# Experts' second product with one 512-column matmul for two passes, the sum finished outside TensorE

## The chip, the cores and the metric

The kernel runs on one core of a Trainium2 chip. The metric is the device time of one execution in microseconds (us). Before the change it is 3690.21 us, the median of three runs (3688.73 to 3691.08). The change is judged by the same metric.

## What is computed

The input is 8 batches of 1024 rows of 256 numbers. Each row is normalised; an attention block gives `s`, a mixture of 8 experts (each row goes to its best two) gives `g`, and the output is `x + s * g`. This case touches the experts alone:

```
buf = zeros((E, capacity, H)).at[flat_e, slot].add(dispatched)
h = silu(einsum('ech,ehf->ecf', buf, w1))
out_buf = einsum('ecf,efh->ech', h, w2)
pair_out = out_buf[flat_e, slot] * keep
```

with E = 8 experts, H = 256 and F = 1024.

## The kernel before

**Two parts for each number.** Products are made in a fast 32-bit format (fp32r) that keeps fewer bits. So each operand is split into a high part (the rounded value) and a low part (the rest), and each product is three matmuls: high by high, high by low, low by high. `PASSES` lists the three.

**Groups.** The rows of all experts are cut into 71 groups of 256 rows (`GROUPS`, `GP`), each of one expert. Groups are numbered from 0; "a" below is the group whose first product runs. Every engine has its own program, and they meet through semaphores.

- TensorE (`tensor`, `body`, lines 1834 to 1893): for group a the first product `hidden(a)` (48 matmuls of 256 columns into four banks `phid`), then `turn(a+1)` (four transposes of the next group's rows), then the second product of the group before, `down(a-1)`, again 48 matmuls of 256 columns: two row tiles c, eight pieces f of the inner dimension, three passes. They sum up in the first 256 columns of the two banks `po`. `down` first waits (line 1853) until the sums of the group before have been taken out of `po` (`s_oe`).
- ScalarE, ACT (`scalar`, `body`, line 1803): `high1(a+1,0)` makes the high part of half of the next w1, four times `silu(a,j)` (two instructions each), `high1(a+1,1)`, and `high2(a+1,0)`, `high2(a+1,1)` for w2. `high1` waits for the load of w1 (`s_w1`), `high2` for `down(a-1)`.
- VectorE, DVE (`vector`, `body`, line 1728): `low1(a+1,0)`, four times `hidden(a,j)` (the low part of the silu's result), `turned(a+1)` (two instructions on the transposes), `low1(a+1,1)`, `outputs(a-1)` (line 1723: copies `po` to `out`, raises `s_oe`), `low2(a+1,0)`, `low2(a+1,1)`.
- GpSimd, POOL (`gpsimd`, line 1641) issues all DMAs of this stage, in a fixed order: for group g two scatters of the results of group g-4 to DRAM (`scatter(g - LAG)`, LAG = 4, which waits for `s_oe`), the load of w1 of g (1 MB), two gathers of the rows of g, the load of w2 of g (1 MB). An indirect DMA costs POOL itself about a microsecond, in which it makes the DMA's descriptors.

**The order of POOL's steps for one group:**

```
for g in range(GROUPS):
    if g >= LAG:
        scatter(g - LAG)             # waits for s_oe >= g - LAG + 1
    if g >= 2:
        e.wait_ge(s_w1l, 2 * (g - 1))
    weights(g, io["w1"], raw1[q], s_w1[q])
```

**The end.** After the loops, ACT and DVE already make the parts of the attention's first output pieces (`first_piece`, lines 1752 to 1766 and 1819 to 1824), as their loads land; TensorE runs `hidden(70)`, `down(69)`, `down(70)` and the first products of the next phase.

Of the kernel before, what the change touches and what calls it, by code (L numbers as in the profile page):

```python
# [24 lines left out]
P = 128  # L25
NBATCH, S, D = 8, 1024, 256
# [56 lines left out]
class Phase:  # L83
# [5 lines left out]
    def sb(self, name, shape, dt=F32):  # L89
        return self.ctx.enter_context(self.nc.sbuf_tensor(f"{self.tag}_{name}", shape, dt))  # L90
# [1462 lines left out]
def expert_parts(nc, ctx, bridge, io, scr, keep, seam):  # L1553


    with ExitStack() as tiles:
# [18 lines left out]
        w1[1] = sb("w11", [P, HL, NF, KD, P], F32R)  # L1575
        w2[1] = sb("w21", [P, HL, NF, D], F32R)
        hT[1] = sb("hT1", [P, HL, NF, GP], F32R)
        phid = ps("h", [P, NQ, HALF])
        ptr = ps("tr", [P, KD, HALF])
        po = ps("o", [P, GT, HALF])  # L1580
# [1 line left out]
        s_rows = sem("rows")  # L1582
        s_slots, s_tr, s_xh, s_xT, s_h, s_silu, s_hT, s_o, s_oe = (sem(n) for n in ("slots", "tr", "xh", "xT", "h", "act", "hT", "o", "oe"))
        s_w1h, s_w1l, s_w2h, s_w2l = (sem(n) for n in ("w1h", "w1l", "w2h", "w2l"))
        s_wo, s_wh, s_wl = (sem(n) for n in ("wo", "wh", "wl"))

        def half1(tile, k):
            return tile[:, k * (W // 2):(k + 1) * (W // 2)]
# [10 lines left out]
        def groups(e, body, after=None):  # L1599

            for g in range(3):
                body(At(0, g))
                if after:
                    after(g)
            with e.Fori(1, (GROUPS - 1) // 2 - 1) as it:
                for off in (1, 2):
                    body(At(it, off))

        def first_piece(q):

# [104 lines left out]
        def vector(e, after):  # L1715
            low1, low2, turned = vector_steps(e)

            def hidden(a, j):
                fs = slice(2 * j, 2 * j + 2)
                e.wait_ge(s_silu, a.n(2 * NQ, 2 * j + 2))  # L1720
                e.tensor_tensor(out=hT[a.u][:, 1, fs, :], in0=hs[:, fs, :], in1=hT[a.u][:, 0, fs, :].bitcast(F32), op=ALU.subtract).then_inc(s_hT, 1)

            def outputs(a):
                wait(e, s_os[a.u], a.same(16 * GT))
                e.wait_ge(s_o, a.n(1, 1))
                e.tensor_copy(out[a.u][:, :, :], po[:, :, 0:D]).then_inc(s_oe, 1)  # L1726

            def body(a, first=False):
                one = a.next(1)
                if first:  # L1730
                    turned(one)
                low1(one, 0)
                for j in range(NQ):
                    hidden(a, j)
                if not first:
                    turned(one)
                low1(one, 1)
                if not first:
                    outputs(a.next(-1))
                low2(one, 0)  # L1740
                low2(one, 1)

            groups(e, lambda a: body(a, isinstance(a.base, int) and a.off == 0), after)
            body(At(0, GROUPS - 2))
            last = At(0, GROUPS - 1)
            e.wait_ge(s_wh, 1)
            e.tensor_tensor(out=wo[1][:, :, :], in0=wraw, in1=wo[0][:, :, :].bitcast(F32), op=ALU.subtract).then_inc(s_wl, 1)
            for j in range(NQ):
                hidden(last, j)
            outputs(last.next(-1))  # L1750

            def low(q):
                src, hi, lo = first_piece(q)
                e.wait_ge(seam["oh"], q + 1)
                e.tensor_tensor(out=lo, in0=src, in1=hi.bitcast(F32), op=ALU.subtract).then_inc(seam["ol"], 1)

            for q in range(TB // 2):
                low(q)
                if q == 2:
                    e.wait_ge(s_o, GROUPS)  # L1760
                    wait(e, s_os[last.u], last.same(16 * GT))
                    e.tensor_copy(out[last.u][:, 0, :], po[:, 0, 0:D]).then_inc(s_oe, 1)
            e.wait_ge(s_o, GROUPS + 1)
            e.tensor_copy(out[last.u][:, 1, :], po[:, 1, 0:D]).then_inc(s_oe, 1)
            for q in range(TB // 2, TB):
                low(q)

# [23 lines left out]
        def scalar(e):  # L1791
            high1, high2 = scalar_steps(e)

            def silu(a, j):
                fs = slice(2 * j, 2 * j + 2)
                e.wait_ge(s_h, a.n(NQ, j + 1))
                wait(e, s_hT, a.n(NQ, j + 1 - NQ))
                if j == 0:
                    wait(e, s_o, a.n(1, -1))
                e.activation(hT[a.u][:, 0, fs, :].rearrange("p f s -> p (f s)"), phid[:, j, :], ACT.Silu).then_inc(s_silu, 1)  # L1800
                e.activation(hs[:, fs, :].rearrange("p f s -> p (f s)"), phid[:, j, :], ACT.Silu).then_inc(s_silu, 1)  # L1801

            def body(a):
                one = a.next(1)
                high1(one, 0)
                for j in range(NQ):
                    silu(a, j)
                high1(one, 1)
                high2(one, 0)
                high2(one, 1)  # L1810

            groups(e, body)
            body(At(0, GROUPS - 2))
            e.wait_ge(s_wo, 16)
            e.activation(wo[0][:, :, :], wraw, ACT.Copy).then_inc(s_wh, 1)
            for j in range(NQ):
                silu(At(0, GROUPS - 1), j)
            e.wait_ge(s_h, NQ * (GROUPS - 1))
            for q in range(TB):
                if q == TB // 2:  # L1820
                    e.wait_ge(s_o, GROUPS - 1)
                e.wait_ge(seam["o"][q // 2], 16)
                src, hi, lo = first_piece(q)
                e.activation(hi, src, ACT.Copy).then_inc(seam["oh"], 1)
# [9 lines left out]
        def tensor(e, after, emptied):  # L1834
            def hidden(a, after=None):
                q = a.u
                e.wait_ge(s_xT, a.n(1, 1))
                for j in range(NQ):
                    if j % 2 == 0:
                        e.wait_ge(s_w1l, a.n(2, j // 2 + 1))  # L1840
                    wait(e, s_silu, a.n(2 * NQ, 2 * j + 2 - 2 * NQ))
                    for f in (2 * j, 2 * j + 1):
                        for ws, xs in PASSES:
                            for k in range(KD):
                                mm = e.matmul(phid[:, j, f % 2 * GP:(f % 2 + 1) * GP], w1[q][:, ws, f, k, :], xT[q][:, xs, k, :],  # L1845
                                              start=(ws + xs + k == 0), stop=(ws == 1 and k == KD - 1))
                    mm.then_inc(s_h, 1)
                    if j == 0 and after:
                        after()

            def down(a, halves=False):
                q = a.u
                wait(e, s_oe, a.n())
                for c in range(GT):
                    for f in range(NF):
                        if c == 0 and f % 2 == 0:
                            e.wait_ge(s_hT, a.n(NQ, f // 2 + 1))
                        if c == 0 and f % (NF // 2) == 0:
                            e.wait_ge(s_w2l, a.n(2, f // (NF // 2) + 1))
                        for hh, ws in PASSES:  # L1860
                            mm = e.matmul(po[:, c, 0:D], hT[q][:, hh, f, c * P:(c + 1) * P], w2[q][:, ws, f, :],  # L1861
                                          start=(hh + ws + f == 0), stop=(hh == 1 and f == NF - 1))
                    if halves and c == 0:
                        mm.then_inc(s_o, 1)
                mm.then_inc(s_o, 1)

            def body(a):
                first = isinstance(a.base, int) and a.off == 0
                if first:
                    turn(e, a.next(1))  # L1870
                hidden(a, after if first else None)
                if not first:
                    turn(e, a.next(1))
                if first:
                    emptied()
                else:
                    down(a.next(-1))

            groups(e, body)
            body(At(0, GROUPS - 2))  # L1880
            last = At(0, GROUPS - 1)
            hidden(last)
            down(last.next(-1))
            down(last, True)
            e.wait_ge(s_silu, 2 * NQ * GROUPS)
            e.wait_ge(s_wl, 1)
            for t in range(READY):
                if t % 2 == 0:
                    e.wait_ge(seam["ol"], t + 2)
                for r in range(HP):  # L1890
                    for os, ws in PASSES:
                        e.matmul(seam["pj"][t][:, 0:D], seam["oT"][0][os][:, r, t * P:(t + 1) * P], wo[ws][:, r, :],
                                 start=(os + ws + r == 0), stop=(os == 1 and r == HP - 1))
# [421 lines left out]
```

## Time and profile before

| | us |
|---|---|
| median of three runs | 3690.21 |
| the profiled execution's own time | 3694.65 |
| its span (first to last instruction) | 3693.1 |
| PE busy | 3626.7 (98%) |
| DVE busy | 3198.4 (87%) |
| ACT busy | 2773.1 (75%) |
| POOL busy | 1198.0 (32%) |
| mean granted clock of TensorE | 0.997 of full speed |

The experts' stage lies between about 2650 and 3500 us from the span's start. In a row of the timeline the columns are the start, the duration, the engine, the line, the operation, what is written and read, the shape, and how many instructions were merged; behind them, in brackets, how long the engine was idle before and what ended that. PE stands for matmuls, PEld for TensorE's weight loads.

### The profile page before, as it was taken

To read this page: it belongs to the slowest core of one execution; us is meant where nothing else is said; L and a number is where in the kernel's file an instruction comes from. 1 tells how busy PE (TensorE), PEld (TensorE's weight loads), DVE (VectorE), ACT (ScalarE), POOL (GpSimd) and SP (SyncE) were. 2 spreads that over 40 slices of the span, in tenths; PEclk is the share of its full clock that TensorE was granted. 3 is DMA by queue.
4 is the path that set the end of the run, shared out by engine and by line. 5 is a ranking of instruction groups with operands and counts; after the bars stand their busy time and mean duration, and the time that the engine had idled before them with its cause. 6 is when DMAs were issued, how large, how long until landed. Compare 5 with 4: busy or idle time off the path is not lost. (4 is left out here: it accounts for less than half of the span.)

```text
span 3693.1 us, 76388 instructions
## 1 busy us (share of the span) xinstructions
PE 3626.7 (98%) x23848; PEld 2352.4 (64%) x23848; DVE 3198.4 (87%) x4340; ACT 2773.1 (75%) x4016; POOL 1198.0 (32%) x1178
## 2 busy tenths in 40 slices
PE   6989999999999999999999999999999999999999
PEld 5754444444444444444444444444699999999998
DVE  8868999999999999999999989999777777777799
ACT  5767888888888888887888888888766666666665
POOL 2202222222222222222222222223366666666400
PEclk9999999999999999999999999999999999999999
DMA  7975666666666666666666666665566666666798
GB/s 261 358 262 136 175 167 173 170 168 171 163 174 160 181 160 181 155 183 157 180 160 174 166 173 170 166 170 147 169 218 224 219 214 216 224 214 216 234 370 274
DMA packets 378435, 724.72 MB, mean 196 GB/s; under 512 B 105277, under 2 KB 253886, under 8 KB 342272
## 3 DMA queue, kind: packets, MB, share of 16 engines
q0 software_dynamic: 83504, 340.66, 35.8%
q1 hardware_dynamic: 292816, 382.71, 31.3%
q10 hardware_dynamic: 2048, 0.53, 0.1%
q8 instruction: 34, 0.56, 0.1%
q14 instruction: 33, 0.27, 0.0%
HBM read 453.60 MB, written 138.81 MB: 160 GB/s over the span
## 5 line engine op out<-in xcount | busy, mean ns | idle before, releaser
L1161 ACT ACTIVATE at_ex<-at_st 128x1024 f32<-128x1024 f32 x1024 | 1049.7, 1026 | 114.6 <-PE at_st L1326 101.3
L1339 PE MATMUL at_pv<-at_ex,at_v 128*64 128x512 f32 x4096 | 991.6, 605 | 0.0
L1019 DVE TENSOR_REDUCE at_mx<-at_fr 128x1 f32<-128x512 f32 x1024 | 705.4, 689 | 238.1 <-PE at_fr L1349 195.6
L1185 ACT ACTIVATE at_fr<-at_fr 128x512 f32<-128x512 f32 x1024 | 602.7, 589 | 290.2 <-PE at_fr L1349 244.9
L1339 PEld LDWEIGHTS at_pv<-at_ex,at_v 128*64 128x64 f32 x4096 | 248.4, 136 | 478.4 <-issue 463.0
L1032 DVE TENSOR_TENSOR at_sum<-at_sum,at_ex 128x1024 f32<-128x1024 f32 x448 | 544.9, 1216 | 3.7 <-ACT at_ex L1161 2.4
L1349 PE MATMUL at_fr<-at_kfar,at_qh 64*128 64x512 f32 x1024 | 460.0, 449 | 5.5 <-DVE at_mx L1019 5.0
L1346 PE MATMUL at_fr<-at_kdif,at_qh 64*128 64x512 f32 x1024 | 460.3, 449 | 3.5 <-DVEq L674 2.5
L1346 PEld LDWEIGHTS at_fr<-at_kdif,at_qh 64*128 64x128 f32 x1024 | 188.1, 184 | 416.4 <-issue 362.7
L1861 PE MATMUL ex_o<-ex_w,ex_hT 128*128 128x256 f32 x3408 | 426.0, 285 | 0.9 <-DVE ex_out L1726 0.9
L1845 PE MATMUL ex_h<-ex_xT,ex_w 128*128 128x256 f32 x3408 | 421.1, 283 | 1.8 <-ACT ex_hs L1801 1.5
L1845 PEld LDWEIGHTS ex_h<-ex_xT,ex_w 128*128 128x128 f32 x3408 | 414.1, 192 | 3.0 <-issue 2.6
L1861 PEld LDWEIGHTS ex_o<-ex_w,ex_hT 128*128 128x128 f32 x3408 | 413.2, 192 | 1.1 <-DVE ex_out L1726 1.1
L1326 PE MATMUL at_st<-at_qh,at_kh 64*128 64x512 f32 x2048 | 407.4, 394 | 5.4 <-DMA at_top<-at_mneg 5.1
L1326 PE MATMUL at_st<-at_ql,at_kh 64*128 64x512 f32 x2048 | 402.7, 389 | 0.0
L1326 PE MATMUL at_st<-at_qh,at_kl 64*128 64x512 f32 x2048 | 402.6, 389 | 0.0
L920 POOL DMA_DIRECT2D at_rotq<-at_swpq x126 | 111.4, 1031 | 842.2 <-DVE at_swpq L987 841.5
L1779 ACT ACTIVATE ex_w<-seam_stage 128x1024 fp32r<-128x1024 f32 x142 | 142.6, 1051 | 286.1 <-PE ex_o L1861 286.1
L1651 POOL DMA_INDIRECT scr_eo<-ex_out,mid_slots x142 | 253.2, 1783 | 215.6 <-DVE ex_out L1726 179.6
L1032 DVE TENSOR_TENSOR at_sum<-at_ex 128x1024 f32<-128x1024 f32 x224 | 272.4, 1216 | 1.7 <-ACT at_ex L1161 1.7
L914 POOL DMA_DIRECT2D at_sum<-at_sum x95 | 88.5, 931 | 519.2 <-DVE at_sum L1032 495.1
L1326 PEld LDWEIGHTS at_st<-at_qh,at_kl 64*128 64x128 f32 x2048 | 193.1, 185 | 45.6
(208 smaller groups left out, 6119.7 us busy)
## 6 DMA issues: line engine op xcount, KB each, us to landing
at_cq<-scr_c SPq DMA_DIRECT2D x62, 1024.0 KB, 6.3
at_ck<-scr_c SPq DMA_DIRECT2D x62, 1024.0 KB, 5.1
at_sum<-at_sum POOLq DMA_DIRECT2D x95, 512.0 KB, 6.1
scr_v<-pj_v SPq DMA_DIRECT2D x64, 512.0 KB, 6.9
at_v<-scr_v SPq DMA_DIRECT2D x64, 512.0 KB, 6.6
mid_rec<-scr_rec SPq DMA_DIRECT2D x256, 128.0 KB, 3.0
scr_o<-mid_oT SPq DMA_DIRECT2D x64, 512.0 KB, 3.1
at_rotq<-at_swpq POOLq DMA_DIRECT2D x126, 256.0 KB, 4.8
```

The costliest lines, as they stand in the source:

```text
L1019: e.reduce_max(mx[k // QB][:, h * QB + k % QB:h * QB + k % QB + 1], fr[h][:, :], AX.X).then_inc(s_tr[h], 1)
L1032: e.tensor_tensor(out=acc, in0=ex[k - 1][:, :, :] if first else acc, in1=ex[k][:, :, :], op=ALU.add).then_inc(s_sum, 1)
L1161: e.activation(ex[k][:, :, :], st[u % 2][:, :, :], ACT.Exp, scale=SCALE).then_inc(s_exp, 1)
L1185: e.activation(fr[h][:, :], fr[h][:, :], ACT.Relu).then_inc(s_pos[h], 1)
L1326: mm = e.matmul(st[u % 2][:, h, :], kk[rows[h], :] if t == 3 else kk[rows[h], keys], qq[rows[h], bank[n]], start=(t == 0 and kt < 2), stop ...
L1339: mm = e.matmul(pv[n][rows[h], :], v[i.u][:, kt, rows[h]], ex[kt][:, h, :], start=(kt == 0), stop=(kt == KT - 1))
L1346: return e.matmul(fr[h][:, :], query_tile(j, k, h), kdif[j.u][rows[h], :], start=True, stop=True)
L1349: return e.matmul(fr[h][:, :], query_tile(j, k, h), kfar[j.u][rows[h], :], start=False, stop=True, skip_group_check=True)
L1651: e.indirect_dma_start(out=scr["eo"], out_offset=bass.IndirectOffsetOnAxis(ap=slots[:, g * GT + c:g * GT + c + 1], axis=0), in_=out[g % 2] ...
L1779: e.activation(w2_half(a.u, 0, k), half2(raw2[a.u], k), ACT.Copy).then_inc(s_w2h, 1)
L1845: mm = e.matmul(phid[:, j, f % 2 * GP:(f % 2 + 1) * GP], w1[q][:, ws, f, k, :], xT[q][:, xs, k, :], start=(ws + xs + k == 0), stop=(ws == ...
L1861: mm = e.matmul(po[:, c, 0:D], hT[q][:, hh, f, c * P:(c + 1) * P], w2[q][:, ws, f, :], start=(hh + ws + f == 0), stop=(hh == 1 and f == NF ...
```

## The change

The operands of two passes, high by high and high by low, share the stationary side (the silu's high part). They become one matmul of 512 columns: the two parts of w2 side by side as the moving operand, into all 512 columns of a `po` bank. The third pass goes on adding to the first 256 columns. The 256 columns of high by low now have to be added afterwards: ACT copies them to a new tile `rest` (`rests`), and DVE's copy to `out` becomes an addition of `po`'s first half and `rest`. `outputs` waits for a new semaphore `s_rest` instead of `s_o`, and both steps have another place: `rests(a-2)` runs on ACT in the body of a, between `silu(a,0)` and `silu(a,1)`, and `outputs(a-2)` on DVE just after `hidden(a,0)`. Before, `outputs(a-1)` stood at the end of the body of a, ahead of `low2(a+1,0)`. POOL's program is not touched.

```
+        def older(a):
+            return not isinstance(a.base, int) or a.n() >= 2
             def outputs(a):
                 wait(e, s_os[a.u], a.same(16 * GT))
-                e.wait_ge(s_o, a.n(1, 1))
-                e.tensor_copy(out[a.u][:, :, :], po[:, :, 0:D]).then_inc(s_oe, 1)
+                e.wait_ge(s_rest, a.n(1, 1))
+                e.tensor_tensor(out=out[a.u][:, :, :], in0=po[:, :, 0:D], in1=rest[:, :, :], op=ALU.add).then_inc(s_oe, 1)
...
                 for j in range(NQ):
                     hidden(a, j)
+                    if j == 0 and older(a):
+                        outputs(a.next(-2))
                 if not first:
                     turned(one)
                 low1(one, 1)
-                if not first:
-                    outputs(a.next(-1))
                 low2(one, 0)
...
             for j in range(NQ):
                 hidden(last, j)
+                if j == 0:
+                    outputs(last.next(-2))
             outputs(last.next(-1))
...
+            def rests(a, c=slice(0, GT), done=1):
+                wait(e, s_oe, a.n(1, done - 1))
+                e.wait_ge(s_o, a.n(1, done))
+                e.activation(rest[:, c, :], po[:, c, D:], ACT.Copy).then_inc(s_rest, 1)
...
                 for j in range(NQ):
+                    if j == 1 and older(a):
+                        rests(a.next(-2))
                     silu(a, j)
...
             for q in range(TB):
                 if q == TB // 2:
-                    e.wait_ge(s_o, GROUPS - 1)
+                    rests(last.next(-1))
+                if q == TB // 2 + 2:
+                    rests(last, slice(0, 1))
+                if q == TB // 2 + 3:
+                    rests(last, slice(1, 2), 2)
...
-                        for hh, ws in PASSES:
-                            mm = e.matmul(po[:, c, 0:D], hT[q][:, hh, f, c * P:(c + 1) * P], w2[q][:, ws, f, :],
-                                          start=(hh + ws + f == 0), stop=(hh == 1 and f == NF - 1))
+                        cols = slice(c * P, (c + 1) * P)
+                        e.matmul(po[:, c, :], hT[q][:, 0, f, cols], w2[q][:, :, f, :], start=(f == 0), stop=(f == NF - 1))
+                        mm = e.matmul(po[:, c, 0:D], hT[q][:, 1, f, cols], w2[q][:, 0, f, :], start=False, stop=(f == NF - 1), skip_group_check=True)
```

The last group's two row tiles are likewise copied and added one by one, and an unused tile of 928 numbers a partition is put ahead of `rest`.

## Rows read from the trace of the kernel before

**Rows 1.** The page, costliest groups: instructions, busy us, mean ns, idle before.

```profile
L1861 PEld LDWEIGHTS ex_o<-ex_w,ex_hT 128*128 128x128 f32 x3408 | 413.2, 192 | 1.1 <-DVE ex_out L1726 1.1
```

**Rows 2.** Sums of one stretch: length, each engine's busy time (instructions), clock, DMA.

```profile
2700.00:3460.00 760.00, 760.00 (x6360) 760.00 (x6359) 584.25 (x698) 496.06 (x764) 499.41 (x381) 1.00 0.63 218
```

**Rows 3.** Waits, 2690 to 3470 us: who for whom, total us, times, longest.

```profile
POOL scr_eo L1651 <- DVE ex_out L1726: 168.2, 66, 2.7
```

**Rows 4.** Timeline of all engines, one group's round, group 30.

```profile
3000.53 5.92 PE L1845 MATMUL ex_h<-ex_xT,ex_w 128*128 128x256 f32 x48
3000.73 2.01 ACT L1779 ACTIVATE ex_w<-seam_stage 128x1024 fp32r<-128x1024 f32 x2 [4.16 <-PE ex_o L1861]
3000.73 0.69 DVE L1726 COPY ex_out<-ex_o 128x512 f32<-128x512 f32 x1 [1.92 <-PE ex_o L1861]
3001.82 2.36 DVE L1683 TENSOR_TENSOR ex_w<-seam_stage,ex_w 128x1024 fp32r<-128x1024 f32 x2 [0.40 <-ACT ex_w L1779]
3002.26 1.67 POOL L1651 DMA_INDIRECT scr_eo<-ex_out,mid_slots  x1 [2.57 <-DVE ex_out L1726]
3002.64 1.04 ACT L1773 ACTIVATE ex_w<-seam_stage 128x1024 fp32r<-128x1024 f32 x1
3003.59 0.57 ACT L1800 ACTIVATE ex_hT<-ex_h 128x512 fp32r<-128x512 f32 x1
...
3004.10 1.22 DVE L1679 TENSOR_TENSOR ex_w<-seam_stage,ex_w 128x1024 fp32r<-128x1024 f32 x1
3004.23 1.95 POOL L1651 DMA_INDIRECT scr_eo<-ex_out,mid_slots  x1 [0.30 <-issue]
3004.55 0.59 ACT L1800 ACTIVATE ex_hT<-ex_h 128x512 fp32r<-128x512 f32 x1
3005.02 0.61 ACT L1801 ACTIVATE ex_hs<-ex_h 128x512 f32<-128x512 f32 x1
3005.23 2.09 DVE L1721 TENSOR_TENSOR ex_hT<-ex_hs,ex_hT 128x512 fp32r<-128x512 f32 x3
...
3006.49 0.98 POOL L1643 DMA_INDIRECT seam_stage<-in_w,keep_widx  x1 [0.30 <-issue]
3006.62 5.82 PEld L1861 LDWEIGHTS ex_o<-ex_w,ex_hT 128*128 128x128 f32 x48
...
3007.61 0.69 DVE L1721 TENSOR_TENSOR ex_hT<-ex_hs,ex_hT 128x512 fp32r<-128x512 f32 x1 [0.28 <-ACT ex_hs L1801]
3007.77 1.37 POOL L1666 DMA_INDIRECT mid_xg<-scr_xn,mid_rows  x1 [0.30 <-issue]
...
3009.55 1.21 DVE L1679 TENSOR_TENSOR ex_w<-seam_stage,ex_w 128x1024 fp32r<-128x1024 f32 x1
3010.70 0.95 POOL L1643 DMA_INDIRECT seam_stage<-in_w,keep_widx  x1 [0.30 <-issue]
...
3014.59 1.05 ACT L1773 ACTIVATE ex_w<-seam_stage 128x1024 fp32r<-128x1024 f32 x1
```

**Rows 5.** Timeline of PE alone: matmuls of 512 columns, back to back.

```profile
207.32 1.52 PE L1423 MATMUL at_fr<-at_cq,at_kdif 128*128 128x512 f32 x6
208.68 1.52 PE L1385 MATMUL at_pv<-at_ck,at_wk 128*128 128x512 f32 x6
```

**Rows 6.** Line 1643, issue to landing: all 2700 to 3470, then w1's of Rows 4.

```profile
DMA to landing us min/median/max: 5.3/5.5/7.9
DMA to landing us min/median/max: 5.5/5.5/5.5
```

**Rows 7.** Timeline of DVE, the low parts of group 2.

```profile
2673.49 2.53 DVE L1721 TENSOR_TENSOR ex_hT<-ex_hs,ex_hT 128x512 fp32r<-128x512 f32 x4
```

**Rows 8.** Timeline of the stage's end: outputs(69), down(70), ACT's third and fourth piece.

```profile
3490.45 0.69 DVE L1726 COPY ex_out<-ex_o 128x512 f32<-128x512 f32 x1 [2.98 <-PE ex_o L1861]
...
3491.19 5.81 PEld L1861 LDWEIGHTS ex_o<-ex_w,ex_hT 128*128 128x128 f32 x48 [1.06 <-DVE ex_out L1726]
...
3492.60 2.01 ACT L1824 ACTIVATE seam_oT<-seam_stage 128x1024 fp32r<-128x1024 f32 x2 [1.11 <-DMA seam_stage<-scr_o]
```

More of the change, by code:

```diff
@@ L1577, in expert_parts @@
         hT[1] = sb("hT1", [P, HL, NF, GP], F32R)
+        sb("past_sums", [P, 928])
+        rest = sb("rest", [P, GT, D])
         phid = ps("h", [P, NQ, HALF])
@@ L1584, in expert_parts @@
         s_w1h, s_w1l, s_w2h, s_w2l = (sem(n) for n in ("w1h", "w1l", "w2h", "w2l"))
-        s_wo, s_wh, s_wl = (sem(n) for n in ("wo", "wh", "wl"))
+        s_wo, s_wh, s_wl, s_rest = (sem(n) for n in ("wo", "wh", "wl", "rest"))
         def half1(tile, k):
@@ L1759, in vector @@
                 if q == 2:
-                    e.wait_ge(s_o, GROUPS)
                     wait(e, s_os[last.u], last.same(16 * GT))
-                    e.tensor_copy(out[last.u][:, 0, :], po[:, 0, 0:D]).then_inc(s_oe, 1)
-            e.wait_ge(s_o, GROUPS + 1)
-            e.tensor_copy(out[last.u][:, 1, :], po[:, 1, 0:D]).then_inc(s_oe, 1)
+                    e.wait_ge(s_rest, GROUPS)
+                    e.tensor_tensor(out=out[last.u][:, 0, :], in0=po[:, 0, 0:D], in1=rest[:, 0, :], op=ALU.add).then_inc(s_oe, 1)
+            e.wait_ge(s_rest, GROUPS + 1)
+            e.tensor_tensor(out=out[last.u][:, 1, :], in0=po[:, 1, 0:D], in1=rest[:, 1, :], op=ALU.add).then_inc(s_oe, 1)
             for q in range(TB // 2, TB):
@@ L1815, in scalar @@
             e.activation(wo[0][:, :, :], wraw, ACT.Copy).then_inc(s_wh, 1)
+            last = At(0, GROUPS - 1)
             for j in range(NQ):
-                silu(At(0, GROUPS - 1), j)
+                if j == 1:
+                    rests(last.next(-2))
+                silu(last, j)
             e.wait_ge(s_h, NQ * (GROUPS - 1))
```

## Prediction

> **What bounds the kernel now.** I read four views. The page's costliest groups show the second product's weight loads, 192 ns each, with 1.1 us of idle time before them in the whole run [rows 1]. The sums over 2700 to 3460 us show PE busy for all 760 us at full clock, while DVE is busy for 584, ACT for 496 and POOL for 499 [rows 2]. So in the experts' stage PE alone sets the pace; its count of instructions and their spacing are the time. The waits show who has room: POOL waits 66 times, 2.5 us each, for the copy on line 1726 [rows 3]. The timeline of one round shows the rest [rows 4]: ACT's `high1(a+1,0)` starts at 3002.64 and that of the next group at 3014.59, so a round is 11.95 us. Two chains cross a round with little room. First, `outputs` to scatter to w1's load to `high1`: w1 of group a+2 is issued at 3006.49, lands 5.5 us later [rows 6] at 11.96, and is wanted at 14.59; room 2.6 us. Second, `outputs` to `down`.
>
> **What the change takes from PE.** 48 loads of `down` last 5.82 us; less the last one's own 0.19, over 47 steps, that is 0.120 us a matmul of 256 columns [rows 1, 4]. Matmuls of 512 columns on full 128x128 weights start every (208.68 - 207.32)/6 = 0.227 us [rows 5]. Three matmuls of 0.120 become 0.227 + 0.120: 0.347 in place of 0.360 us, 0.013 less, as one change of weights goes and the columns stay 768. There are 16 such triples a group and 71 groups: 0.21 us a round, 15.1 us in all. That the moving operand now comes in two runs of 256 is not in any row; bounds are no gain at all (two steps of 0.120, near which it would only come if the split cost 13 ns) and the 0.227. I take the 0.227, the same shape. If PE stayed the bound, a round would be 11.74 us.
>
> By the Trainium skill, "TensorE: Matmul & The Clock Gate", section "Back-to-back issue gap", a warm matmul takes N/2.4 + 2.5 ns, so 109 and 216 ns. The rows have 120 and 227, about 11 ns more each. By the page the merger would save 2.5 ns a triple, 2.8 us in all.
>
> **What it adds.** ACT: one copy of 128x512 a round. Its neighbours of that size start 0.48 apart (3004.55, 3005.02) [rows 4]. It runs beside PE, and ACT idles 4.16 us a round [rows 4]: nothing by itself. DVE: the addition reads `po` and `rest`; the copy took 0.69 us, and like-sized additions last 0.69 too (3007.61) [rows 4]; nothing. `rests` waits for `s_o` of a `down` that ended before `high2`, so it never blocks ACT. It starts 0.95 us after `silu(a,0)` does and is done before DVE comes to the addition (below).
>
> **What it moves, and who is queued behind.** `outputs(a-2)` ran at 3000.73, right after `down(a-2)`. It now runs behind `low2`, `low1(a+1,0)` and `hidden(a,0)`. `hidden(a,0)` starts at 3005.23, and steps of DVE of this size follow one another after 0.60 us ((2.53 - 0.69)/3 with a first wait left out, [rows 7]). So the addition starts at 3005.83, 5.1 us later than the copy. Call this moment O.
> - PE's `down(a-1)` waits for its end, O + 0.69 + 0.05 = 3006.57 (0.05: end of the copy 3491.14 to PEld 3491.19 [rows 8]), plus the sequencer's steps behind the wait. PE gets there at 3006.62: a delay of 0 to 0.2 us a round, at most 14 us.
> - POOL's scatter waits for it too, and in POOL's program w1's load of group a+2 stands behind the two scatters. Here the 5.1 us meet a room of 2.6. This is where the time goes.
>
> **The new loop.** `outputs(n)` releases `scatter(n)`, behind it w1 of n+4 is loaded, `high1(n+4,0)` waits for it on ACT, `silu(n+3,0)` is queued behind `high1`, `hidden(n+3,0)` on DVE waits for both, and the next thing on DVE is `outputs(n+1)`. Once around per group, independent of PE. From O:
> - the addition, 0.69; to POOL's scatter 3002.26 - 3001.42 = 0.84 [rows 4]: O + 1.53.
> - POOL's own time. An indirect DMA takes 0.95 us when DVE is idle (3010.70). The scatters took 1.67 and 1.95 and the gather 1.37 [rows 4]. The excess of each is just the time until DVE's running operation on two SBUF tiles is over: 3002.26 to the second `low2` at about 2.96 is 0.70; 4.23 to 5.23 is 1.00; 7.77 to 8.21 is 0.44. So I lay POOL against DVE's new order. ACT's `high1` starts at O - 2.83 (below); silu pairs follow 0.95 after it and 0.95 apart, with 0.48 for `rests` after the first pair, and the second pair's result is there 1.1 us after its start: O + 0.66. So `hidden(a,1)` starts near O + 0.69, (2) near 1.67, (3) near 2.64 (the same steps on), each for 0.60. The first scatter (O + 1.53) meets none: 0.97. The next starts 0.30 after, O + 2.80, and waits for `hidden(a,3)` until 3.24: ends 4.19. w1's load starts at O + 4.50. `low1(a+1,1)`, which would hold it for 1.14 us, follows `hidden(a,3)` by 9.55 - 7.61 = 1.94 [rows 4], at O + 4.58: 0.08 us too late to catch it.
> - landing 5.5 [rows 6]: O + 10.00. To ACT's start 0.1: bounded by 0.03 (ACT to DVE) and 0.84 (DVE to POOL), near the first, as a compute engine waits.
> - `high1` to `low1` on DVE 1.09 (3000.73 to 3001.82), `low1` to `hidden(.,0)` 1.13, to the addition 0.60 [rows 4]: 2.83.
>
> Sum: 4.50 + 5.5 + 0.1 + 2.83 = 12.93 us, more than 11.74. The loop is the bound, and PE's gain and the added work vanish in its room.
>
> **The sum.** `outputs(0)` comes with group 2, at 2673.49 + 0.60 = 2674.09 [rows 7]. 67 loops lead to `outputs(67)`: 2674.09 + 67 x 12.93 = 3540.4. `down(68)` follows after 0.69 + 0.15 at 3541.2; before, it started 39 rounds after `down(29)`, the one in rows 4 (3006.62 + 39 x 11.95 = 3472.8). Later by 68.4. Behind it `down(68)` is 0.2 shorter. At the end `rests(69)` stands behind ACT's fourth piece, while the copy of 69 did not: the pieces start at 3492.60, wait for a load and take 1.9; `rests(69)` 3494.5 to 3495.1, addition to 3495.85, `down(70)` at 3495.9 in place of 3491.19 [rows 8]: 4.7 later (`down(69)` waits too, for `outputs(68)`, but less than this covers). Together 72.9: 3694.65 + 72.9 = 3767.6 for an execution like the profiled one, which is 4.4 above the median of the runs. So 3763 us.
>
> **The rivals.**
> 1. *A longer loop.* POOL is caught once more, by `low1(a+1,1)` (margin 0.08 us) or by `hidden(a,2)`: 1.1 us more, 14.0 a round, 67 x 1.07 = 72 more: 3835. For it: the margins are thin; some loads took up to 7.9 to land [rows 6].
> 2. *A shorter loop.* The second scatter isn't caught (margin 0.16 us): 12.4 to 12.5, 3690.2 + 36 + 4.5 = 3731.
> 3. *Faster: w1's load still lands in time.* One mechanism: the loop stays below 11.74, PE remains the bound. Then 15.1 less, the end's 4.7 more, some 2 for `down` behind `outputs`: 3682. It decides at 1.2 us less than my sum. Against it: with POOL never caught (3.5 to 4.0 up to w1) and the shortest landing of 5.3 the loop is still 12.2.
> 4. *No change: a quick landing.* If w1 landed 1.1 us sooner, in 4.4, the loop would be 11.83 and the time 3690. No load of line 1643 took under 5.3 [rows 6]. The 4.4 us is what the Trainium skill gives for 1 MB, "DMA: Bandwidth & Descriptors", section "Anatomy of one DMA — SWDGE (gpsimd) path" (2.0 us and the bytes at 436 GB/s); by that rule the change would cost nothing; the trace disagrees by 1.1 us.
> 5. *PE's clock falls* in the 1.2 us it now idles a round. At the lower of its two levels for a third of its work PE would need 3.9 us more, and could become the bound at 15.7 a round: 67 x 2.7 = 181 more, 3944. Clock is 1.00 in the stretch [rows 2]; nothing there speaks for it.
>
> **How the numbers follow.** Forecast 0.45, longer loop 0.25, shorter 0.18, faster 0.05, no change 0.03, clock 0.04. The range takes in the first three: 3724 to 3842. A measurement of this kernel can tell about 0.2% from no change: faster 0.05, same 0.03, slower 0.92.
>
> **What would show it.** After the change ACT should wait at line 1773 for w1's load, 1.2 us or more in each round; PE should idle as much a round, ahead of `down`, released by line 1726's successor on DVE; POOL's wait for DVE should be there still, and the rounds in the timeline be 12.9 apart. 512-column matmuls should start 0.227 apart. The chain is wrong if w1 lands before ACT wants it; only the sizes are if ACT waits but the round isn't 12.9.

## The result, and the profile after

The changed kernel takes 3772.9 us (median of 4 runs, 3772.2 to 3775.7) where the kernel before takes 3690.6 on the same chip: 1.0221 times as long, with a 95% interval of 1.0209 to 1.0233. It is 82 us slower, though TensorE has less to do. The profiled execution took 3772.2 us with a span of 3770.6; that of before 3694.65 and 3693.1. The difference of the two spans, 77.5 us, is what the traces can account for.

In the changed kernel the lines have moved: `outputs` is L1731, the hidden layer's low parts L1726, `low1` L1684, `low2` L1688, `high1` L1780, `high2` L1786, `rests` L1813, the scatters L1656, the loads of w1 and w2 L1648, the second product L1882 (512 columns) and L1883 (256).

The sums over the stretch of [rows 2], 2700 to 3460 us (length; busy time of PE, PEld, DVE, ACT, POOL with instructions; clock; share and GB/s of the DMA engines):

```profile
2700.00:3460.00 760.00, 702.78 (x4881) 647.73 (x4880) 539.32 (x640) 487.03 (x755) 403.97 (x349) 1.00 0.56 199
```

PE was busy for all 760 us before and is now idle for 57 of them. Every engine does less in the same time: DVE 539 instead of 584, POOL 404 instead of 499. No engine has become the bound; they all wait for one another. The waits of 2690 to 3540 us (who for whom: us in all, times, longest), which answer to [rows 3]:

```profile
POOL scr_eo L1656 <- DVE ex_out L1731: 297.2, 65, 5.7
...
ACT ex_w L1780 <- DMA seam_stage<-in_w,keep_widx: 81.2, 60, 2.5
DVE ex_w L1684 <- ACT ex_w L1780: 65.3, 62, 3.4
PE ex_o L1882 <- DVE ex_out L1731: 61.7, 62, 2.5
```

The last three are new (among the eight longest waits of before, over 2690 to 3470 us, there is none of ACT for w1's load, none of DVE for `high1` and none of PE for `outputs`), and they are one chain: ACT waits for w1's load, DVE for ACT, PE for DVE. POOL in turn waits for DVE, and issues w1's load behind that; so the chain bites its own tail. One turn of it in the timeline, DVE, POOL, ACT and PE put together as in [rows 4] (start, duration, engine, line, in brackets the idle time before and what ended it). `outputs` runs at 3000.46 and again at 3013.28:

```profile
3000.46 0.68 DVE L1731 TENSOR_TENSOR ex_out<-ex_o,ex_rest 128x512 f32<-128x512 f32 x1
...
3001.98 1.01 POOL L1656 DMA_INDIRECT scr_eo<-ex_out,mid_slots  x1 [4.37 <-DVE ex_out L1731]
3003.29 1.38 POOL L1656 DMA_INDIRECT scr_eo<-ex_out,mid_slots  x1 [0.30 <-issue]
3004.97 0.98 POOL L1648 DMA_INDIRECT seam_stage<-in_w,keep_widx  x1 [0.30 <-issue]
...
3005.05 1.21 DVE L1684 TENSOR_TENSOR ex_w<-seam_stage,ex_w 128x1024 fp32r<-128x1024 f32 x1
...
3010.45 1.06 ACT L1780 ACTIVATE ex_w<-seam_stage 128x1024 fp32r<-128x1024 f32 x1 [1.12 <-DMA seam_stage<-in_w,keep_widx]
...
3013.28 0.68 DVE L1731 TENSOR_TENSOR ex_out<-ex_o,ex_rest 128x512 f32<-128x512 f32 x1
...
3014.21 0.47 PE L1882 MATMUL ex_o<-ex_w,ex_hT 128*128 128x512 f32 x1 [0.73 <-DVE ex_out L1731]
```

From `outputs` to w1's load 4.51 us, to ACT's `high1` 5.48, to `outputs` again 2.83: 12.82. The room of 2.6 us between w1's landing and ACT's need of it, read from [rows 4, 6], is gone, and ACT has 1.12 us of idle time in its place. Over the 67 turns of the stage the four legs have these medians and means: `outputs` to the start of w1's load 4.51 and 4.57 us, landing 5.52 and 5.60, landing to `high1` 0.10 and 0.07, `high1` to `outputs` 2.84 and 2.85. The means sum to 13.09, which is (3546.03 - 2669.15)/67.

### The profile page after: what moved, and what is told of

Same layout as the page of the kernel before. It is cut to its first block and busy times, and to the rows that moved or that the text cites. A ratio compares the mean times of both kernels' runs of the same rounds, so it can differ in the third digit from the quotient of the medians.

```text
span 3770.6 us, 74292 instructions
## 1 busy us (share of the span) xinstructions
PE 3638.8 (97%) x22712; PEld 2297.1 (61%) x22712; DVE 3203.0 (85%) x4340; ACT 2815.2 (75%) x4088; POOL 1134.1 (30%) x1178
## 5 line engine op out<-in xcount | busy, mean ns | idle before, releaser
L1882 PE MATMUL ex_o<-ex_w,ex_hT 128*128 128x512 f32 x1136 | 413.1, 406 | 69.2 <-DVE ex_out L1731 69.2
L1883 PE MATMUL ex_o<-ex_w,ex_hT 128*128 128x256 f32 x1136 | 320.3, 282 | 0.0
L1786 ACT ACTIVATE ex_w<-seam_stage 128x1024 fp32r<-128x1024 f32 x142 | 142.7, 1052 | 231.0 <-PE ex_o L1883 231.0
L1882 PEld LDWEIGHTS ex_o<-ex_w,ex_hT 128*128 128x128 f32 x1136 | 215.9, 190 | 133.2 <-issue 45.3
L1688 DVE TENSOR_TENSOR ex_w<-seam_stage,ex_w 128x1024 fp32r<-128x1024 f32 x142 | 167.8, 1222 | 150.2 <-ACT ex_w L1786 150.2
L1656 POOL DMA_INDIRECT scr_eo<-ex_out,mid_slots x142 | 169.9, 1197 | 361.6 <-DVE ex_out L1731 323.0
```

Source lines behind the costliest of these rows:

```text
L1656: e.indirect_dma_start(out=scr["eo"], out_offset=bass.IndirectOffsetOnAxis(ap=slots[:, g * GT + c:g * GT + c + 1], axis=0), in_=out[g % 2] ...
L1882: e.matmul(po[:, c, :], hT[q][:, 0, f, cols], w2[q][:, :, f, :], start=(f == 0), stop=(f == NF - 1))
L1883: mm = e.matmul(po[:, c, 0:D], hT[q][:, 1, f, cols], w2[q][:, 0, f, :], start=False, stop=(f == NF - 1), skip_group_check=True)
```

## The experiments

Two theories stood against each other. *The loop*: the later `outputs` closes a loop over POOL's fixed order, w1's load and DVE, which no engine's work sets; the merged product is harmless. *The work*: the rounds are longer because ACT's copy, the addition and the wider matmul cost more than they save. Each kernel's time is a median beside the kernel before on its own chip, which was at 3690.1 (for the first four of the table), 3689.8 (the next four) and 3692.8 (the last two); so compare the ratios across chips, not the times. "Round" is the median from one hidden layer's first matmul to the next; that of before is 11.953 us.

| kernel | us | ratio, 95% interval | round, us |
|---|---|---|---|
| moved, not merged | 3806.4 | 1.0315 [1.0298, 1.0333] | 13.593 |
| merged, not moved | 3686.8 | 0.9992 [0.9982, 1.0001] | 11.847 |
| changed, w1's load halved | 3707.3 | 1.0045 [1.0028, 1.0061] | 12.013 |
| changed, scatters a group later | 3693.5 | 1.0007 [0.9997, 1.0017] | 11.954 |
| changed, a fill on POOL | 3836.5 | 1.0397 [1.0378, 1.0416] | 14.076 |
| before, the same fill | 3689.5 | 0.9998 [0.9988, 1.0008] | 11.953 |
| merged, not moved, w2 side by side | 3686.1 | 0.9992 [0.9983, 1.0001] | 11.847 |
| merged, not moved, earlier last copy | 3683.0 | 0.9980 [0.9971, 0.9989] | 11.847 |
| changed, w1's load ahead of the scatters | 3699.6 | 1.0015 [1.0005, 1.0025] | 11.921 |
| as the row "earlier last copy", matmuls grouped | 3683.2 | 0.9970 [0.9960, 0.9981] | 11.787 |

**Only the move.** The kernel before, with nothing changed but the place of `outputs`:

```
                 for j in range(NQ):
                     hidden(a, j)
+                    if j == 0 and (not isinstance(a.base, int) or a.n() >= 2):
+                        outputs(a.next(-2))
...
                 low1(one, 1)
-                if not first:
-                    outputs(a.next(-1))
```

> The kernel before with nothing but the place of the copy changed: outputs(a-2) right after hidden(a,0) on DVE; no 512-column matmul, no rest. Loop theory (the copy's late place delays scatter and with it the load of w1): slow, without any of the new arithmetic. Laid out as in the prediction, without ACT's extra copy hidden(a,1) to (3) come 0.1 to 0.5 us earlier against O, the first scatter is caught by hidden(a,2) until O+1.8, w1's load starts at O+4.36 and is caught by low1(a+1,1) until O+5.17: loop 13.6 to 13.7 us, time 3805 to 3815, slower than the changed kernel itself. If DVE's running operation doesn't hold POOL (rival on the size): loop 12.9 to 13.1, 3765 to 3773. Rival (the cost is the new work: 512 columns out of two runs, the extra ACT copy, two inputs for DVE): 3690 to 3700.

Measured 3806.4: the move alone costs 116 us, more than the whole change. So the merged product, ACT's copy and the addition don't lengthen the rounds; in the new place they even shorten them by 0.66 us (13.593 to 12.935). POOL's and DVE's timeline of this kernel shows why (`outputs` is L1726 here and had started 4.37 us before the load, `low1` is L1679):

```profile
3001.80 1.22 DVE L1679 TENSOR_TENSOR ex_w<-seam_stage,ex_w 128x1024 fp32r<-128x1024 f32 x1
...
3002.07 1.79 POOL L1643 DMA_INDIRECT seam_stage<-in_w,keep_widx  x1 [0.30 <-issue]
```

Here `low1` starts 0.27 us ahead of w1's load, and the load takes POOL 1.79 us in place of 0.98, until `low1` is over. The landing, counted from the load's start, has a median of 6.31 us in place of 5.52: 0.79 more. In the changed kernel ACT's copy after the first silu pair holds up the pairs behind it by 0.48 us, and with them `hidden(a,1)` to `hidden(a,3)` and `low1` on DVE, which then comes 0.08 us after the load. By these rows an added operation on ACT made the round shorter; no run adds the copy alone.

**Only the merge.** The changed kernel with `rests` behind `high1(a+1,1)` and `outputs` where it was before:

```
                 for j in range(NQ):
-                    if j == 1 and older(a):
-                        rests(a.next(-2))
                     silu(a, j)
                 high1(one, 1)
+                if older(a.next(1)):
+                    rests(a.next(-1))
```

> The changed kernel with the merged matmul, the copy to rest and the addition, but the latter two in the old place (outputs(a-1) ahead of low2(a+1,0), rests(a-1) just ahead of high2(a+1,0)). Loop theory: PE is the bound again, 11.74 us a round: 15 us less than before, plus some 4 at the end (rests(69) behind ACT's fourth piece): 3680, ratio 0.997. If the merged matmul saves nothing: 3695. Rival (the new work costs the time): 3770 as after the change.

The loop is open: every round takes 11.847 us, PE is busy for 760 of 760 us. But the gain per round is 0.106 us and not 0.21, and the end loses 6.0 us: from the last hidden layer to the first matmul of the next product it is 24.4 us, 18.4 before. Both were followed up below. What is left of the time, 3.3 us less than before, can't be told from nothing: the interval takes in 1.

**A microsecond on POOL inside the loop.** A fill of a spare tile, from group 8 on, in both kernels:

```
                     scatter(g - LAG)
+                if g > 8:
+                    e.wait_ge(s_slots, 16 + g - 8)
+                if g >= 8:
+                    e.memset(spare[:, :], 0.0).then_inc(s_slots, 1)
                 if g >= 2:
```

> The changed kernel with one POOL fill of a spare tile of 928 columns (about 1.2 us with its gap, an estimate) between the two scatters and the load of w1, from group 8 on; the output is unchanged. Theory 'loop outputs, scatters, w1 load, landing, high1, low1, hidden, outputs': every microsecond on POOL between the scatters and the load is on the loop: a round of 13.09 + about 1.2 = 14.3, 62 rounds, 3772.9 + 75 = 3848 (3825 to 3870, since the size of the fill is an estimate). Rival 'the rounds are longer because DVE, ACT or the DMA queues carry more': POOL has 13.09 - 4.9 us free in a round, the fill is hidden, 3773.

> The kernel before with the same fill at the same place, which separates its price as work from its price on the loop. Theory: the loop isn't closed there (the w1 load is early by more than a microsecond against its reader), 3690 and a round of 11.95. Rival: it lengthens the rounds here too, by up to 1.2 us each, 3765; then the change didn't put the load on the path, it was there before.

The fill takes 0.89 us. Rows of the changed kernel, POOL's and DVE's, and POOL's of the kernel before:

```profile
3009.56 0.89 POOL L1666 MEMSET ex_past_sums<- 128x928 f32 x1
...
3009.93 1.21 DVE L1688 TENSOR_TENSOR ex_w<-seam_stage,ex_w 128x1024 fp32r<-128x1024 f32 x1
...
3010.61 1.39 POOL L1648 DMA_INDIRECT seam_stage<-in_w,keep_widx  x1 [0.16 <-issue]
```

```profile
3004.64 0.89 POOL L1662 MEMSET ex_spare<- 128x928 f32 x1
3005.69 0.99 POOL L1644 DMA_INDIRECT seam_stage<-in_w,keep_widx  x1 [0.16 <-issue]
```

The fill follows the second scatter at once, and 0.16 us lie behind it where 0.30 lay between scatter and load. So it puts the load off by 0.89 + 0.16 - 0.30 = 0.75 us in both kernels (median from `outputs` to the load 5.26 in place of 4.51, and 6.51 in place of 5.76). In the changed kernel the later load also meets `low1`, and takes POOL 1.39 us in place of 0.98. The two together are 1.16, and the median round grew by 1.14. In the kernel before the same 0.75 us are free: 3689.5, round 11.953 to the nanosecond. So the stretch of POOL's program between `outputs` and w1's load is on the path after the change, and was not before.

The time grew by 63.6 us (3836.5 - 3772.9), near what 62 fills of 1.05 us would give, but that isn't how it came about: 63 turns have a fill, 47 us of fills in all, and the load caught by `low1` in 61 of them adds 25 more. Against that the profiled execution of this kernel lacks most of the late turns of the changed kernel, described further below. The forecast's 3848 had 1.2 us for the fill and left the catch out.

**Half the load.** The changed kernel, w1's load cut to half its bytes from group 4 on (its first half then holds other rows' numbers and the rest is stale, so the output is wrong; order and waits stay):

```
-                weights(g, io["w1"], raw1[q], s_w1[q])
+                if g < 4:
+                    weights(g, io["w1"], raw1[q], s_w1[q])
+                else:
+                    weights(g, io["w1"].rearrange("r (h c) -> (r h) c", h=2), raw1[q][:, 0:W // 2], s_w1[q])
```

> The changed kernel with w1's load halved from group 4 on (the first half of the tile alone is loaded, with wrong rows, and the rest keeps an older group's numbers); order and waits stay. Loop theory: landing falls from 5.5 to about 3.6 us, the loop to about 11.0, under PE's 11.74: 3680 to 3692. Rival (the landing is not in the loop; PE, ACT or DVE themselves are slower): 3770.

It lands 1.5 us sooner (median of the 24 loads whose landing is recorded and that `low1` didn't hold: 3.98), and 65 of the 82 us come back, so the landing is a leg of the loop. But 3707 was not in the forecast of 3680 to 3692. The turns alternate between 11.86 to 11.97 and 12.1 to 12.3. POOL's and DVE's rows of a long one:

```profile
3011.54 1.22 DVE L1687 TENSOR_TENSOR ex_w<-seam_stage,ex_w 128x1024 fp32r<-128x1024 f32 x1
...
3011.81 1.80 POOL L1648 DMA_INDIRECT seam_stage<-in_w,keep_widx  x1 [0.30 <-issue]
```

With the loop shorter, `low1` again starts ahead of the load and lengthens it by 0.8 us, in every second round. A halved load also lands in 3.98 and not in 3.6.

**The loop opened by a later scatter.** The changed kernel with the scatters one group later (`LAG` 5 in place of 4), which frees w1's load from the group's `outputs`:

```
-        HL, LAG = 2, 4
+        HL, LAG = 2, 5
```

> The changed kernel with LAG = 5: POOL scatters the group before the one it scatters now, so that it never waits for the moved addition; all arithmetic and the late place stay. Loop theory: the loop is cut, PE is the bound at 11.74 plus 0 to 0.2 for down behind outputs: 3676 + 0 to 14 + 4 at the end, 3680 to 3692, centre 3685. Rival (PE waits for the late addition, or the new work costs): 3770.

All but 3.4 us of the 82 come back, PE is busy for 760 of 760 us again. The round's mean is 11.925, 0.08 above that of "only the merge": between a hidden layer's last matmul and the second product's first there are 590 ns in place of 475, the wait behind the late `outputs`. The rest is one long round at the start (16.1 us) and 4.3 us at the end, so it came out a little above the forecast.

**The loop opened by POOL's order.** The changed kernel, each load of w1 ahead of the scatters:

```
             for g in range(GROUPS):
                 q = g % 2
-                if g >= LAG:
-                    scatter(g - LAG)
                 if g >= 2:
                     e.wait_ge(s_w1l, 2 * (g - 1))
                 weights(g, io["w1"], raw1[q], s_w1[q])
+                if g >= LAG:
+                    scatter(g - LAG)
```

> The changed kernel, where POOL issues each load of w1 ahead of the two scatters instead of behind them; copy and addition stay where the change put them. Theory 'the loop runs through POOL's order': the load of w1 no longer waits for outputs of the group, so it starts 4 to 5 us earlier against its reader, the loop is open by far more than the 1.1 us it was too long, and the rounds go back to TensorE's work, 11.85, with at most 0.1 us for the late outputs; with the end's +4, 3685 to 3697, centre 3692. Rival 'outputs is late because of what stands ahead of it on VectorE, whatever POOL does': the round stays at 13 and the time at 3773.

```profile
3005.22 0.94 POOL L1648 DMA_INDIRECT seam_stage<-in_w,keep_widx  x1 [0.30 <-issue]
```

The load starts 2.9 us ahead of `outputs` (3008.14) instead of 4.5 behind it; `high1` no longer waits for it, and the round is 11.92. So DVE's order by itself, which is that of the changed kernel, costs 0.07 us a round, not 1.1. The kernel is still 0.15% slower than before: the late `outputs` (613 ns in place of 475 ahead of each second product), a first long round (2.9 us more) and the end (3.9 us more) outweigh the 0.106 us a round that the merge saves. The forecast's 3697 at most was for a chip on which before takes 3690; by the ratio this is 3695.7.

**Why 0.106 us and not 0.21.** In "only the merge" the 512-column matmul takes 236 ns from start to start (median of 1136; most are 232 to 241) and the 256-column one 117, together 353 (in the changed kernel, where the loop is the bound, the median is 233), where [rows 5] had given 227 + 120. Two causes were tried. First, w2's parts side by side, so that the 512 columns are one run (`w2` as `[P, NF, HL, D]` in place of `[P, HL, NF, D]`):

```
-        w2[0] = sb("w20", [P, HL, NF, D], F32R)
+        w2[0] = sb("w20", [P, NF, HL, D], F32R)
...
-            return half2(w2[q][:, s, :, :].rearrange("p f d -> p (f d)"), k)
+            return w2[q][:, k * (NF // 2):(k + 1) * (NF // 2), s, :]
...
-                        e.matmul(po[:, c, :], hT[q][:, 0, f, cols], w2[q][:, :, f, :], start=(f == 0), stop=(f == NF - 1))
+                        e.matmul(po[:, c, :], hT[q][:, 0, f, cols], w2[q][:, f, :, :], start=(f == 0), stop=(f == NF - 1))
```

> The kernel with the merged product and everything else in its old place (3686.8 us, round 11.847 us), with w2's two parts of one block of rows laid side by side on chip, so that the 512 columns that a matmul streams are one contiguous run instead of two runs of 256. In that kernel and in the changed one the 512-column matmul takes 234 to 241 ns from start to start, where the stage before it had 227. Theory 'the split operand costs it': 227 ns again, a round of 11.74, some 70 rounds x 0.11 = 7.5 us less, 3679. Rival 'it is the neighbour' (a 256-column matmul in between, a new weight load for each): 236 ns and 3687 as before. What would speak for a third case: ScalarE's and VectorE's operations on w2 longer than 0.96 and 1.14 us per half because their output is now in pieces.

Nothing changed: 236 and 117 ns, a round of 11.847. The split of the operand is free. Second, the order of the matmuls, tried together with the earlier last copy of the next experiment:

```
                         e.matmul(po[:, c, :], hT[q][:, 0, f, cols], w2[q][:, :, f, :], start=(f == 0), stop=(f == NF - 1))
+                    for f in range(NF):
                         mm = e.matmul(po[:, c, 0:D], hT[q][:, 1, f, cols], w2[q][:, 0, f, :], start=False, stop=(f == NF - 1), skip_group_check=True)
```

> The kernel with the merged product in the old place and the earlier last copy (3683.0, round 11.847), where in each column of tiles the eight 512-column matmuls go first and the eight 256-column ones behind them, instead of in turn. It tells what makes the 512-column matmul take 236 ns from start to start instead of the 227 ns of the stage before. Theory 'changing between the two widths costs it': 227 and 120 ns, 0.347 per triple, round 11.74, 70 x 0.107 = 7.5 us less, 3675.5. Rival 'a 512-column matmul that writes two runs of the accumulator with a new weight load costs 236 ns anyway, and the 256 one behind it gets 3 ns back': 0.356 per triple, a round of 11.9, 3686.

It fell between the two: 231 ns (median, 226 to 236) among 512-column ones, 120 for the others, a round of 11.787. So the alternation costs about 4 ns of the 6 or 7 missing per triple (0.060 us by 16 triples); what the other 3 are for stays open. The time is 3683.2 against 3692.8, the best ratio of the study (0.9970); against the 0.9980 of the earlier last copy alone the intervals overlap.

**The end.** In "only the merge" the copy of the second half of `outputs(69)` stands on ScalarE behind four pieces of the next product, and runs at 3485.55:

```profile
3483.64 2.00 ACT L1841 ACTIVATE seam_oT<-seam_stage 128x1024 fp32r<-128x1024 f32 x2 [1.02 <-DMA seam_stage<-scr_o]
...
3486.23 0.69 DVE L1731 TENSOR_TENSOR ex_out<-ex_o,ex_rest 128x512 f32<-128x512 f32 x1 [6.19 <-ACT ex_rest L1811]
```

Moved ahead of the third piece:

```
             for q in range(TB):
-                if q == TB // 2:
+                if q == 2:
                     rests(last.next(-1))
```

> The kernel with everything in its old place (3686.8), where the 6.0 us that it loses after the last hidden layer come from the copy of the second half of outputs(69), which stands on ScalarE behind four pieces that wait for transfers (copy at 3485.55, addition at 3486.23 after 6.19 us idle, down(70) behind it). Here that copy stands ahead of the third piece: down(69) ends at 3482.2, copy 3482.4 (or at 3482.6, behind the second piece), addition 3483.1 to 3483.3, down(70) from 3483.9 instead of 3487.0. Theory: 3.1 us come back, 3683.7. Rival: the first product's pieces end last anyway, nothing comes back, 3687; if all 6.0 were that one copy, 3681.

3683.0. On the same chip "w2 side by side", which has the rounds of "only the merge", took 3686.1, 3.1 us more; the two intervals just overlap. `outputs(69)` now comes 12.4 us after the last hidden layer's start in place of 15.5, the 3.1 us foreseen, and the next product's first matmul 18.8 in place of 24.4. Why 5.6 us there are worth only some 3 in the time stays open. This version is faster than the kernel before by 0.2% (interval 0.1 to 0.3%).

## Why the prediction was right, point by point

**The verdict and its mechanism.** 3763 us was forecast, 3724 to 3842, slower with 0.92; 3772.9 came. The mechanism is the one described: the loop through POOL's order, shown by four edits at POOL's stretch of it: the fill makes it longer (+63.6 us, and nothing in the kernel before), the halved load shorter, the later scatter and the earlier load open it. ACT waited for w1's load 60 times, 1.35 us each, much as the forecast's list of signs has it.

**The loop's legs.** The forecast had 4.50 + 5.5 + 0.1 + 2.83 = 12.93. The medians are 4.51, 5.52, 0.10 and 2.84, and the median round is 12.935. Even the order laid out by hand held: the first scatter was not caught (1.01 us), the second was, by `hidden(a,3)`, and took 1.38 for the forecast's 1.39; w1's load escaped `low1` by 0.08 us, at 3004.97 against 3005.05.

**Where it was off: the late turns.** 67 turns took 876.9 us, where 67 x 12.93 is 866.3: 10.6 more. The forecast summed a typical turn, but a turn's late leg adds and nothing subtracts. Twelve turns exceed 13.15 us, and they hold all of it. The tail of [rows 6], up to 7.9 us, is not the reason: counted from the end of POOL's own instruction, 66 of the 67 loads landed within 4.39 to 4.76 us. What was late was mostly POOL and PE:
- POOL stood still. In the turn of `outputs(16)` 2.09 us lay between the scatters in place of 0.30, and the second then met `low1` and took 1.99: that turn took 15.39. In those of `outputs(33)` and `outputs(50)` 0.88 us lay ahead of the load, which then met `low1` too (1.57 us in place of 0.98). These three are 4.8 us of the 10.6. The halved load's kernel is late in the same three turns; what POOL did there is open.
- PE's clock fell. At 2684.1, 2895.7 and 2923.0 it was at the lower level for a few microseconds, each time just behind a long turn (14.41, 15.39 and 13.87 us) in which PE had idled for 1.9 to 3.2 us; the long turns of `outputs(33)` and `outputs(50)` had no fall behind them. `outputs` then came 3.1 to 3.2 us after `high1` in place of 2.84, and in the turn behind each, `low1` started some 0.3 us ahead of the load, which took 1.80 us. These six turns are 4.1 us.
- The first turn was 1.5 us late: POOL took 1.42 us for the load, and it is the only one that landed late (5.66 us after POOL's instruction). The last two of the twelve landed at 5.71 and 5.74 us and make 0.5.

The stretch of one fall (length, busy times, clock, DMA), and POOL's rows of the longest turn and of the load of the turn behind the fall:

```profile
2895.70:2899.20 3.50, 3.50 (x13) 2.92 (x13) 2.92 (x5) 2.14 (x4) 2.79 (x3) 0.51 0.15 55
```

```profile
2883.57 1.99 POOL L1656 DMA_INDIRECT scr_eo<-ex_out,mid_slots  x1 [2.09 <-issue]
...
2912.24 1.80 POOL L1648 DMA_INDIRECT seam_stage<-in_w,keep_widx  x1 [0.30 <-issue]
```

So the forecast's rival 1 (a load caught once more) and rival 5 (the clock) did happen, in a few turns each; it weighed them as fates of the whole stage and had nothing for them in the sum.

**The start.** `outputs(0)` came at 2669.15, 4.9 us before the forecast's 2674.09. Attention ended sooner in this execution, which is 3.1 us of it: the first hidden layer starts anywhere from 2639.1 to 2644.7 in the twelve traces (2643.8 before, 2640.7 after), so that part is scatter between executions. The other 1.8 us lie between the first hidden layer and `outputs(0)` and weren't traced. Together they hid half of the miss above: `outputs(67)` was at 3546.03 for 3540.4.

**The end.** The sum had 4.5 us more from `down(68)` on; 4.0 came (77.93 us later at `down(70)`, 73.97 at `down(68)`). The path was another one. The forecast let `rests(69)` wait for ACT's fourth piece. In fact `down(69)` itself was late, behind wo's subtraction on DVE and `outputs(68)`, and then ran for 3.4 us at a granted clock of 0.52, that is at the lower of its two levels, 1.2 GHz; pairs of matmuls started 0.64 us apart in place of 0.35. The sums of that stretch, then ACT's next copy:

```profile
3561.20:3564.60 3.40, 3.40 (x13) 2.89 (x12) 0.73 (x2) 2.00 (x2) 0.97 (x1) 0.52 1.10 348
```

```profile
3567.68 0.60 ACT L1813 ACTIVATE ex_rest<-ex_o 128x512 f32<-128x512 f32 x1 [0.86 <-PE ex_o L1883]
```

`rests(69)` waited for `down(69)` (0.86 us), and the piece ahead of it was done. That the number fits is chance. The forecast's mechanism does exist: in "only the merge", where `down(69)` is on time, it costs 6 us.

**What was subtracted for the median.** The profiled execution of before lay 4.4 us above its median, and the forecast took that off. The changed kernel's profiled execution lies 0.7 below its own. The sum for an execution, 3767.6, missed by 4.6; these 5.1 make it 9.7, or 9.9 from the rounded 3763.

**PE's saving.** Forecast 13 ns a triple, measured 7, in the kernel with the place kept: the 512-column matmul takes 236 ns there. As forecast, the loop swallowed it, so the term weighed nothing. Had the rival "faster" come true, 3682 would have been 7 us too low; with the place kept, 3686.8 was measured.

**The added work.** ACT's copy (0.60 us) and the addition (0.68) cost nothing as work, as said; but the copy wasn't neutral. It is what keeps `low1` off w1's load. Without it the loop is 13.59: this is rival 1, "POOL is caught once more", with 0.79 us in place of the 1.1 foreseen. A margin of 0.08 us decided between 3773 and some 3817 (67 times 0.66 more). The forecast gave it 0.25. (Both figures rest on the rows of "only the move", where the merge is missing too.)

**The other rivals.** PE idled about 1.0 us in each turn (57.2 of 760), and the clock's mean over 2700 to 3460 reads 1.00, but it did fall three times within the 67 turns, as above, and once at the end. With the fill on POOL PE idled 88.8 of the 760 us and the mean was 0.97. In neither kernel did PE become the bound. No load of w1 landed in 4.4 us; the fastest of 67 took 5.37. Against rival 3 the forecast set a loop of 12.2 with POOL never caught, "3.5 to 4.0 up to w1". By its own steps that stretch is 1.53 + 0.97 + 0.30 + 0.95 + 0.30 = 4.05, the loop then 12.3, and the argument stands; with 3.5 the loop would be 11.7 and it would not. PE's delay behind the late `outputs`, 0 to 0.2 us a round in the forecast, can be read where the loop is open: 0.115 (590 - 475 ns) and 0.138 (613 - 475).

## What to carry to other kernels

A step moved on one engine moves everything that other queues issue behind it. Follow the moved step's semaphore to the queue that waits on it, list what stands behind that wait in program order, and ask whether any of it feeds the moved step again; if it does, sum the loop's legs and compare them with the busiest engine's round. Here a saving of 0.1 us a round on the bound engine was bought with a loop 1.1 us too long. When the loop is the bound, a typical turn is the floor: each pause of the queue, each catch and each fall of the clock is added, here 0.16 us a turn. Before blaming a landing, take the queue's own instruction off it. Look at margins under 0.1 us as coin tosses. To find out whether a stretch of a queue is on the path, put a microsecond of idle work there, in both kernels, and read from the rows what it really adds: here 0.75 us of its own and 0.41 by the meeting that it caused.

## What the runs showed of the hardware

**POOL's indirect DMAs and DVE's operations on two SBUF tiles.** An indirect DMA takes POOL 0.94 to 1.01 us, and longer by just the time until such an operation of DVE is over, if one is running when it starts. Over 2700 to 3460 us of the twelve traces 1536 of these instructions started with no such operation running, and none took over 1.02 us; 2044 started with one running and took over 1.1 us, and ended 0.82 to 0.97 us after it; some 820 more started so near its end that little was left to wait for. Another 51 started within 0.04 us of the operation's own start and weren't held. Single cases: 1.79 and 1.80 us with 1.22 us long `low1` started 0.27 us ahead, 1.38 with `hidden(a,3)` (3003.11 to about 3003.72) against a start at 3003.29. DVE's cast and subtraction of `turned`, whose first input is in PSUM, ran from 3003.72 to 3005.05 and lengthened nothing: the second scatter ended at 3004.67, which is 0.95 after `hidden(a,3)`'s end. The Trainium skill has the rule for compute instructions, "SBUF — State Buffer", section "Who interferes with whom": a DVE instruction with two inputs in SBUF contends with a GpSimd instruction that reads SBUF. It infers that such an instruction leaves descriptor generation alone; the rows here disagree, by 0.4 to 0.8 us in the cases named.

**A 512-column matmul depends on its neighbours.** 227 ns among its like in [rows 5], 231 in groups of eight that add into one accumulator, 236 when 256-column ones stand between (233 where the loop is the bound). Whether the moving operand is one run of 512 columns or two of 256 made no difference (236 ns both ways).

**Half a megabyte lands in 3.98 us where a whole one takes 5.5**, when POOL's instruction isn't held. Counted from that instruction's end it is 3.01 and 4.53 us: the second half megabyte costs 1.5 us.
